# One feed-forward stage of an eight-stage kernel: the activation clip moved from VectorE to ScalarE, the 8-bit rounding read from PSUM, and a quarter of the last butterfly level moved into TensorE's Hadamard product

## The reference

```
def act_quant(x):                      # per token, 8 bits
    scale = 128 / clip(max|x|, 1e-5)
    return clip(round(x * scale), -128, 127) / scale
def weight_quant(w):                   # ternary, one scale
def fwht(x):                           # Walsh-Hadamard over the last axis, h = 1, 2, 4 ... n/2
    a, b = pairs at distance h;  x = [a + b, a - b];  ...;  x / sqrt(n)

gate = act_quant(x) @ weight_quant(w_gate).T          # 256 -> 1024
up   = act_quant(x) @ weight_quant(w_up).T
mid  = silu(gate) * up
out  = act_quant(fwht(mid)) @ weight_quant(w_down).T  # 1024 -> 256
```

## Time and profile before

| | us |
|---|---|
| three runs | 1581.56, 1587.24, 3211.22 |
| their median | 1587.24 |
| span of the profiled execution | 1593.2 |
| the stage in it, from the first `rstd` to the next stage's first | 263.5 to 420.2 |
| POOL busy in 291 to 404 | 109.0 of 113 |

### The profile page before, as it was taken

The page is one execution under the profiler, slowest core; times in us unless marked ns, Lnnn a source line. Parts: engine busy times, 40 slices in busy tenths (PEclk is TensorE's granted clock), DMA queues, the critical chain, the costliest instruction groups (busy, mean ns, idle before and its releaser), DMA issues. The chain is left out here.

```text
span 1593.2 us, 29325 instructions
## 1 busy us (share of the span) xinstructions
PE 1359.9 (85%) x7991; PEld 850.6 (53%) x7992; DVE 1047.0 (66%) x2409; ACT 795.0 (50%) x2354; POOL 633.9 (40%) x658
## 2 busy tenths in 40 slices
PE   5889995778689697999979999888995999968993
PEld 3555552555444253675545666564663666654661
DVE  5898886787568746224648888844334888864224
ACT  4676763666500045331028888723442888833330
POOL 3113411999477313760021111114435664214661
PEclk9999997999899689999979999958997999998997
DMA  5130002300100230985100000421442111412224
GB/s 188 49 107 23 22 9 94 122 0 0 53 0 0 60 115 14 287 283 173 52 28 23 23 26 22 163 64 47 130 121 80 48 53 33 172 54 63 83 82 165
DMA packets 96447, 124.80 MB, mean 78 GB/s; under 512 B 11117, under 2 KB 76464, under 8 KB 96112
## 3 DMA queue, kind: packets, MB, share of 16 engines
q1 hardware_dynamic: 85760, 95.80, 18.9%
q0 software_dynamic: 10608, 28.07, 6.1%
HBM read 91.31 MB, written 33.43 MB: 78 GB/s over the span
## 5 line engine op out<-in xcount | busy, mean ns | idle before, releaser
L717 ACT ACTIVATE l0a_prob<-l0a_ps_s,l0a_neg_max 128x128 f32<-128x128 f32 x512 | 137.9, 398 | 70.8 <-DVE l0a_neg_max L559 63.2
L717 ACT ACTIVATE l2a_prob<-l2a_ps_s,l2a_neg_max 128x128 f32<-128x128 f32 x512 | 138.7, 402 | 26.7 <-DVE l2a_neg_max L559 22.0
L1160 ACT ACTIVATE l3a_prob<-l3a_ps_s,l3a_neg_max 128x256 f32<-128x256 f32 x256 | 104.5, 483 | 33.0 <-DVE l3a_neg_max L1074 31.5
L219 POOL TENSOR_TENSOR ln_rstd<-ln_var_eps,minus_half 128x4 f32<-128x4 f32 (+1 forms) x14 | 23.1, 1656 | 238.9 <-POOLq L183 208.7
L559 DVE TENSOR_REDUCE l2a_neg_max<-l2a_ps_s 128x4 f32<-128x512 f32 x128 | 85.7, 684 | 20.5 <-PE l2a_ps_s L815 19.6
L502 POOL TENSOR_TENSOR l2a_k_head<-l2a_kT,head_of_row 128x512 f32<-128x512 f32 x32 | 33.1, 1054 | 158.0 <-DMA l2a_kT<-k_rows 158.0
L568 DVE COPY l0a_probT<-l0a_ps_t 128x512 f32<-128x512 f32 x128 | 84.7, 683 | 14.5 <-PE l0a_ps_t L827 14.4
L1074 DVE TENSOR_REDUCE l3a_neg_max<-l3a_ps_s 128x2 f32<-128x512 f32 x128 | 84.0, 680 | 13.4 <-PE l3a_ps_s L1211 12.4
L559 DVE TENSOR_REDUCE l0a_neg_max<-l0a_ps_s 128x4 f32<-128x512 f32 x128 | 85.5, 683 | 8.2 <-PE l0a_ps_s L815 7.5
L502 POOL TENSOR_TENSOR l0a_k_head<-l0a_kT,head_of_row 128x512 f32<-128x512 f32 x32 | 32.6, 1040 | 137.9 <-DMA l0a_kT<-k_rows 137.9
L1819 PE MATMUL l1a_ps_y<-l1a_kv,l1a_tap 128*128 128x512 f32 x192 | 84.1, 601 | 3.7 <-POOL l1a_kv L1791 3.7
(11 more groups left out here) (475 smaller groups left out, 3543.1 us busy)
## 6 DMA issues: line engine op xcount, KB each, us to landing
l1f_w_gu<-in_l1f_w_gu SPq DMA_DIRECT2D x32, 352.0 KB, 6.5
expert_results<-zeros SPq DMA_DIRECT2D x1, 8320.0 KB, 26.3
l1f_got<-expert_results SPq DMA_DIRECT2D x16, 512.0 KB, 4.4
expert_results<-l2f_y_sb SPq DMA_DIRECT2D x47, 128.0 KB, 1.7
l1f_w_d<-in_l1f_w_d SPq DMA_DIRECT2D x32, 176.0 KB
l2f_w_gu_all<-in_l2f_w_gu SPq DMA_DIRECT2D x1, 4096.0 KB, 14.1
l3f_w_gu_all<-in_l3f_w_gu SPq DMA_DIRECT2D x1, 4096.0 KB, 14.0
l3f_got<-expert_results SPq DMA_DIRECT2D x16, 256.0 KB, 5.5
```

The source lines that it names most:

```text
L717: last = act.activation(prob[4 * c + j][:, r * P:r * P + P], ps_s[j][:, r * P:r * P + P], ACT.Exp, bias=neg_max[:, j, r:r + 1])
L1160: last = act.activation(prob[4 * c + j][:, m * D:m * D + D], ps_s[j][:, m * D:m * D + D], ACT.Exp, bias=neg_max[:, j, m:m + 1])
```

## The change

- `clip_x` goes from DVE to ACT. DVE did `min(xr - MAGIC, 127)`; ACT now does `relu(MAGIC + 127 - xr)`, which is 127 minus that value, and the copy of `xqT` out of PSUM (before a plain copy) now does `127 - value`. In ACT's tile it stands last, after `norm`, for tile `t+4`; DVE had it first in its tile, for `t+3`.
- `round_h` writes back into `ps_f` (PSUM) instead of an SBUF buffer, and `quantise_h` on DVE reads `ps_f`. PE may refill `ps_f` only when `hq` is done, where before it was when the rounding was done.
- The two factors `deq` are written by two 128x1 instructions instead of one 128x2. There are two `a_rec` buffers, with a wait of DVE on the rounding two tiles back.
- POOL's levels come in the order 512, 256, 128 columns apart. The last level is done for blocks 0 to 5 only (two instructions of 128x384 instead of 128x512); the difference that becomes blocks 6 and 7 is written straight into `mixed` by the level before. PE does the missing pair: for block 6 it multiplies by `[H H]`, for block 7 by `[H -H]`, each 256 columns wide, summed in PSUM.
- The Hadamard matrix is loaded twice side by side, and ACT makes the negative once, before the stage's first work. Two more constants are set on POOL.

```diff
@@ load_ahead
-        sp.dma_start(core.had[:, :], core.dram["had"]).then_inc(core.had_in, 16)
+        sp.dma_start(core.had[:, 0:2, :], core.dram["had"].unsqueeze(1).broadcast_to([P, 2, P])).then_inc(core.had_in, 16)
@@ POOL
-            pool.memset(magic[:, :], MAGIC).then_inc(const_done, 1)
+            for n, value in ((magic, MAGIC), (clip_at, MAGIC + 127.0), (top_level, 127.0)):
+                pool.memset(n[:, :], value).then_inc(const_done, 1)
...
-                for n, (src, dst) in enumerate(((prod[u], fly), (fly, prod[u]), (prod[u], mixed[u]))):
-                    v, o = (m[:, :].rearrange("p (a two c) -> p a two c", two=2, c=P << n) for m in (src, dst))
-                    if n:
-                        pool.drain()
-                    pool.tensor_tensor(o[:, :, 0, :], v[:, :, 0, :], v[:, :, 1, :], ALU.add)
-                    last = pool.tensor_tensor(o[:, :, 1, :], v[:, :, 0, :], v[:, :, 1, :], ALU.subtract)
-                last.then_inc(mixed_done, 1)
+                even, odd = pairs(prod[u], W4)
+                high, low = pairs(fly[:, :], W4)
+                pool.tensor_tensor(high, even, odd, ALU.add)
+                pool.tensor_tensor(low, even, odd, ALU.subtract)
+                pool.drain()
+                even, odd = pairs(fly[:, :], 2 * P)
+                pool.tensor_tensor(pairs(prod[u], 2 * P)[0], even, odd, ALU.add)
+                pool.tensor_tensor(levels[u][:, :].rearrange("p (n c) -> p n c", c=2 * P)[:, 1:8:6, :], even, odd, ALU.subtract)
+                pool.drain()
+                even, odd = pairs(prod[u][:, 0:6 * P], P)
+                high, low = pairs(mixed[u][:, 0:6 * P], P)
+                pool.tensor_tensor(high, even, odd, ALU.add)
+                pool.tensor_tensor(low, even, odd, ALU.subtract).then_inc(mixed_done, 1)
@@ DVE
-                dve.reciprocal(a_rec[:, :], a_max[u][:, :]).then_inc(x_scaled, 1)
-                dve.tensor_scalar(deq[u][:, :], w_mean[:, 0:2], a_max[u][:, :], None, ALU.mult)\
-                   .then_inc(deq_done, 1)
-
-            def clip_x(t):
-                dve.wait_ge(x_rounded, t + 1)
-                if after(t, 1):
-                    dve.wait_ge(xqT_put, t)
-                dve.tensor_scalar(xq[:, :], xr[:, :], MAGIC, 127.0, ALU.subtract, ALU.min).then_inc(xq_done, 1)
+                if after(t, 2):
+                    dve.wait_ge(x_rounded, t - 1)
+                dve.reciprocal(a_rec[u][:, :], a_max[u][:, :]).then_inc(x_scaled, 1)
+                for n in range(2):
+                    dve.tensor_scalar(deq[u][:, n:n + 1], w_mean[:, n:n + 1], a_max[u][:, :], None, ALU.mult)\
+                       .then_inc(deq_done, 1)
...
-                dve.tensor_scalar(hq[:, :], rounded[:, :], MAGIC, 127.0, ALU.subtract, ALU.min).then_inc(hq_done, 1)
+                dve.tensor_scalar(hq[:, :], ps_f[:, :], MAGIC, 127.0, ALU.subtract, ALU.min).then_inc(hq_done, 1)
@@ ACT
+            def clip_x(t):
+                act.wait_ge(x_rounded, t + 1)
+                if after(t, 1):
+                    act.wait_ge(xqT_put, t)
+                act.activation(xq[:, :], xr[:, :], ACT.Relu, bias=clip_at[:, :], scale=-1.0).then_inc(xq_done, 1)
...
-                act.activation(xqT[u][:, :, :].rearrange("p c t -> p (c t)"), ps_xqT, ACT.Copy).then_inc(xqT_done, 1)
+                act.activation(xqT[u][:, :, :].rearrange("p c t -> p (c t)"), ps_xqT, ACT.Identity, bias=top_level[:, :],
+                               scale=-1.0).then_inc(xqT_done, 1)
...
-                if after(t, 1):
-                    act.wait_ge(hq_done, t)
-                act.activation(rounded[:, :], ps_f[:, :], ACT.Identity, bias=magic[:, :], scale=b_rec[:, :])\
+                act.activation(ps_f[:, :], ps_f[:, :], ACT.Identity, bias=magic[:, :], scale=b_rec[:, :])\
                     .then_inc(round_done, 1)
...
                 if ahead(t, 5):
                     norm(t + 5, 1 - u)
+                if ahead(t, 4):
+                    clip_x(t + 4)
@@ PE
-                        pe.wait_ge(round_done, t)
-                for c in range(half * NF // 2, (half + 1) * NF // 2):
-                    last = pe.matmul(ps_f[:, c * P:c * P + P], mixedT[:, c * P:c * P + P], had[:, :], start=True, stop=True)
+                        pe.wait_ge(hq_done, t)
+                for c in range(half * NF // 2, (half + 1) * NF // 2 - 2 * half):
+                    pe.matmul(ps_f[:, c * P:c * P + P], mixedT[:, c * P:c * P + P], had[:, 0, :], start=True, stop=True)
                 if half:
+                    for n in range(2):
+                        last = pe.matmul(ps_f[:, 6 * P:8 * P], mixedT[:, (6 + n) * P:(7 + n) * P],
+                                         had[:, n:n + 2, :].rearrange("p n c -> p (n c)"), start=(n == 0), stop=(n == 1))
                     last.then_inc(had_put, 1)
```

More of the change, by code:

```diff
@@ L143, in __init__ @@
         self.ffn_raw = [self.sb(f"ffn_raw{n}", [P, KC * FF], F32, self.early) for n in range(3)]
-        self.had = self.sb("had_matrix", [P, P], F32, self.early)
+        self.had = self.sb("had_matrix", [P, 3, P], F32, self.early)
         self.w_int = [self.sb(f"w_int{n}", [P, KC * FF], BF16, self.early) for n in range(3)]
@@ L1305, in hadamard_ffn @@
         had = core.had
-        magic = sb("magic", [P, 1])
+        magic, clip_at, top_level = (sb(n, [P, 1]) for n in ("magic", "clip_at", "top_level"))
         xn = [sb(f"xn{u}", [P, D]) for u in range(2)]
@@ L1311, in hadamard_ffn @@
         xqT = [sb(f"xqT{u}", [P, KC, P], BF16) for u in range(2)]
-        a_max, a_rec = [sb(f"a_max{u}", [P, 1]) for u in range(2)], sb("a_rec", [P, 1])
+        a_max, a_rec = ([sb(f"{n}{u}", [P, 1]) for u in range(2)] for n in ("a_max", "a_rec"))
         deq = [sb(f"deq{u}", [P, 2]) for u in range(2)]
@@ L1316, in hadamard_ffn @@
         gate = sb("gate", [P, FF])
-        prod = [sb(f"prod{u}", [P, FF]) for u in range(2)]
+        levels = [sb(f"levels{u}", [P, 2 * FF]) for u in range(2)]
+        prod, mixed = ([b[:, n * FF:n * FF + FF] for b in levels] for n in range(2))
         fly = sb("fly", [P, FF])
-        mixed = [sb(f"mixed{u}", [P, FF]) for u in range(2)]
         mixedT = sb("mixedT", [P, FF])
-        rounded = sb("rounded", [P, FF])
         hq = sb("hq", [P, FF], BF16)
@@ L1339, in hadamard_ffn @@
             "rstd_done", "shift_done", "normed", "x_scaled", "x_rounded"))
-        zeroed = sem("zeroed")
+        zeroed, had_ready = sem("zeroed"), sem("had_ready")
         block = st.enter_context(nc.Block())
@@ L1359, in butterflies, with pairs @@
                     pool.wait_ge(mixT_put, t - 1)
-                for n, (src, dst) in enumerate(((prod[u], fly), (fly, prod[u]), (prod[u], mixed[u]))):
-                    v, o = (m[:, :].rearrange("p (a two c) -> p a two c", two=2, c=P << n) for m in (src, dst))
-                    if n:
-                        pool.drain()
-                    pool.tensor_tensor(o[:, :, 0, :], v[:, :, 0, :], v[:, :, 1, :], ALU.add)
-                    last = pool.tensor_tensor(o[:, :, 1, :], v[:, :, 0, :], v[:, :, 1, :], ALU.subtract)
-                last.then_inc(mixed_done, 1)
+                def pairs(m, width):
+                    v = m.rearrange("p (a two c) -> p a two c", two=2, c=width)
+                    return v[:, :, 0, :], v[:, :, 1, :]
+                even, odd = pairs(prod[u], W4)
[11 more added lines that the diff above has]
+                pool.tensor_tensor(low, even, odd, ALU.subtract).then_inc(mixed_done, 1)
             over_tiles(pool, butterflies)
@@ L1423, in tile @@
             def tile(t, u):
-                if ahead(t, 3):
-                    clip_x(t + 3)
                 if ahead(t, 2):
@@ L1462, in round_x @@
                     act.wait_ge(xq_done, t)
-                act.activation(xr[:, :], xn[u][:, :], ACT.Identity, bias=magic[:, :], scale=a_rec[:, :])\
+                act.activation(xr[:, :], xn[u][:, :], ACT.Identity, bias=magic[:, :], scale=a_rec[u][:, :])\
                     .then_inc(x_rounded, 1)
+            def clip_x(t):
[3 more added lines that the diff above has]
+                act.activation(xq[:, :], xr[:, :], ACT.Relu, bias=clip_at[:, :], scale=-1.0).then_inc(xq_done, 1)
             def copy_xqT(t, u):
@@ L1469, in copy_xqT @@
                     act.wait_ge(up_put, t - 1)
-                act.activation(xqT[u][:, :, :].rearrange("p c t -> p (c t)"), ps_xqT, ACT.Copy).then_inc(xqT_done, 1)
+                act.activation(xqT[u][:, :, :].rearrange("p c t -> p (c t)"), ps_xqT, ACT.Identity, bias=top_level[:, :],
+                               scale=-1.0).then_inc(xqT_done, 1)
             def silu(t, u):
                 act.wait_ge(gate_put, t + 1)
-                act.wait_ge(deq_done, t + 1)
+                act.wait_ge(deq_done, 2 * t + 2)
                 if after(t, 1):
@@ L1512, in tile @@
                     norm(t + 5, 1 - u)
+                if ahead(t, 4):
+                    clip_x(t + 4)
+            act.wait_ge(core.had_in, 16)
```

(9 more changed lines are left out.)

3 lines of the change are left out of this document (removed).

## The result

| | before | with the change |
|---|---|---|
| median of 19 runs each | 1584.56 us | 1600.82 us |
| ratio | | 1.0093, 95% interval 1.0072 to 1.0114 |
| span of the profiled execution | 1593.2 | 1599.1 |
| the stage in it, first `rstd` to the next stage's first | 156.63 | 170.29 |

One run on each side was far slower (3211.22 and 2270.51 us), and the ratio leaves these two out. It makes 14.7 us, with its interval 11.4 to 18.1, on 1584.56; the two medians are 16.3 apart; the forecast was +13.9. The stage in the profile is 13.66 longer.

What follows compares the result with a forecast made beforehand. It took a circle of hand-offs of 8.28 us per tile through ACT, DVE and PE, without POOL, as the bound. 6.4 (clip) + 7.2 - 0.2 (PE) + 0.5 (end) = +13.9 on 1587.2 gave 1601 us, range 1589 to 1612.

Steps and rivals of the forecast that it cites:

- The bound: A circle of hand-offs among ACT, DVE and PE sets the stage's period of 8.28 us; POOL is not in it.
- POOL as the bound: Rival, 10%: the stage follows POOL's 7.12 us per tile, 15 periods x 1.0 = -15 us, total 1572.
- The circle: From second copy of mixedT through silu, product, maximum, reciprocal, rounding, round_x, norm and first copy to the next: 8.28 us.
- POOL and the port costed at nothing: POOL's 8.12 to 7.12 us per tile and DVE's vanished port waits gain nothing, being off the circle.
- Clip on ACT: One more ACT instruction between norm and the first copy: 13 x 0.49 = 6.4 us, bounds 3.6 to 7.8.
- PE: Transform's second half with 256-column products: 0.45 us per tile, 16 x 0.45 = 7.2, less 0.2 in the first tile.
- Rounding in PSUM: round_h on ACT writing PSUM: taken as 0, with bounds of +-3.3 us in all.
- The end: At the stage's end nothing covers the slower quantise_h from PSUM: +0.5 us.
- The third rival: The clock falls, 4%: longer waits keep PE at 1.2 GHz, 15 x 2.5 = 37 us more, total 1638.
- Additions hidden: Rival, 10%: clip and wider PE columns fall in gaps, only the 0.5 us at the end is paid, total 1588.
- A table load per relu: Rival: ACT reloads its table for relu in every tile; excluded by the order, with the unforeseen 2%.

Runs made afterwards that it cites:

- the relief of POOL alone: Kernel before, with POOL's last butterfly level left out on blocks 6 and 7 and nothing put on PE; stage 156.8 us, period 8.28, run ratio 1.0011.
- the clip in a gap: Changed kernel with ACT's clip of tile t+3 put between the two copies of hqT; stage 164.3 us, period 8.70, ratio 1.0028 to the kernel before.
- the butterfly part alone: Kernel before with only POOL's last level on 6 of 8 blocks and PE's two products of 256 columns; stage 163.4 us, period 8.70, ratio 1.0043.
- the three instructions in gaps: Changed kernel with round_x, clip_x and norm moved into ACT's gaps; stage 160.1 us, period 8.09, ratio 1.0024 to the kernel before.
- the first with the early turn: Changed kernel with round_x, clip_x, norm in ACT's gaps, and mixedT's next first half turned and copied early; stage 156.4 us, period 8.04.
- The first with the early turn and the old butterflies: The early-turn kernel with POOL doing the whole last level again and PE's products at 128 columns; stage 152.2 us, period 7.81.
- the two with the cut first: Early-turn kernels with DVE's cut of h ahead of the sum into x: stage 150.0 us with 256-column products, 152.4 with the old butterflies.

## Why the prediction was right

*The bound.* Right, and shown by the relief of POOL alone (+0.2) against the -9 to -10 that POOL as the bound would have given. The circle's length, 8.28, came back in the kernel that left its members alone (8.28) and in the one that, of its members, changed only where the rounding is written (8.27). POOL's row before was less unbroken than it looked: it paused 0.24 before its second tile, and in twelve tiles one of its instructions took 0.45 longer than the others, which in a timeline shows as work and not as a gap:

```profile
343.25 1.72 POOL L1365 TENSOR_TENSOR l0f_prod<-l0f_fly 128x512 f32<-128x512 f32 x1
```

With the cut of `h` from PSUM and the narrow factors alone, the same instruction took 1.27 throughout the steady part, and so it did with the change. So a busy share of 97% held some waiting too; POOL's own work before was about 7.7 us per tile.

*POOL and the port costed at nothing.* Right. The idle time of POOL is 1.78 to 2.05 per steady period, forecast about 2; `deq` is 0.32 for the pair, 194 to 206 ns each in all 32, so it waits nowhere; the cut from PSUM is 1.21 (forecast 1.22). The Trainium skill, SBUF — State Buffer (Who interferes with whom), describes such waits as an exclusive lock on ports that VectorE shares with GpSimd, and leaves out of it a VectorE instruction with at most one SBUF input outside its two-port modes; that the cut of `h` from PSUM is free of them beside a busy POOL agrees (`hq` 1.21 in every period, where the old form took 0.69 alone and 1.02 beside it). Here the waits did not matter.

*Clip on ACT.* The mechanism right, the size too high: 0.39 in the circle, where 0.49 had been taken. The instruction is 0.50 long, not 0.59 as its neighbours, and gives way 0.10 before its end as they do. 12 x 0.39 = 4.7 instead of 6.4. The thirteenth, before the first tile, is there too, 0.40 between clip and copy, but it is not paid: with DVE rid of its own cuts the last rounding in the start came 0.36 earlier, 19.60 us after the stage's start instead of 19.96, and the copy at 21.00 instead of 20.96. The clip alone shows the same (19.58 and 20.98). The prediction had left DVE's relief in the start out. Before, and with the change:

```profile
283.50 0.60 ACT L1463 ACTIVATE l0f_xr<-l0f_xn,l0f_magic,l0f_a_rec 128x256 f32<-128x256 f32 x1 [2.79 <-DVE l0f_a_rec L1382]
```

```profile
286.58 0.60 ACT L1465 ACTIVATE l0f_xr<-l0f_xn,l0f_magic,l0f_a_rec 128x256 f32<-128x256 f32 x1 [2.79 <-DVE l0f_a_rec L1394]
287.58 0.49 ACT L1472 ACTIVATE l0f_xq<-l0f_xr,l0f_clip_at 128x256 bf16<-128x256 f32 x1
287.98 0.57 ACT L1492 ACTIVATE l0f_mixedT<-l0f_ps_t 128x512 f32<-128x512 f32 x1
```

*PE.* 0.43 against 0.45: from the start of the second half to the maximum 1.57 instead of 1.14. 15 x 0.43 = 6.5, where 7.2 less 0.2 was forecast; what the first tile paid is in the 0.18 by which the start grew.

*Rounding in PSUM.* 1.18 against 1.20, and the next instruction on ACT starts 1.10 after it in both: the unknown of +-3.3 was worth nothing. Its bounds came from 0.59 against 0.38 for 256 columns, read as SBUF against PSUM. At least part of that is another thing: the copy of `xqT` went from 0.38 to 0.47 when it was given a bias, still from PSUM.

*The end.* +0.5, as forecast.

*What wasn't in the sum.* The clock fell once more, near the end of the stage. After a stretch of 2 us in which PE was busy for 0.75, the granted clock fell to 0.50, the lower level of 1.2 GHz, at 416 to 418:

```profile
412.00:414.00 2.00, 0.75 (x5) 0.42 (x4) 1.81 (x3) 1.27 (x2) 2.00 (x2) 1.00 0.00 0
414.00:416.00 2.00, 1.33 (x10) 1.27 (x11) 0.02 (x1) 0.60 (x1) 1.86 (x3) 0.88 0.00 0
416.00:418.00 2.00, 2.00 (x10) 1.85 (x9) 0.00 (x0) 0.60 (x1) 0.51 (x1) 0.50 0.00 0
```

The two products of 256 columns took 1.90 there instead of 1.03, and that period is 9.39 long beside 7.72 for the next: +1.6. The kernel before had the upper level at that point of its tail. PE's busy time just before doesn't settle the cause: with the clip in a gap it was busy for 0.76 at 402 to 404, with the clock at 1.00 there and in the next 6 us, and for 0.76 again at 410 to 412, with a fall behind it. The third rival was this, kept to one period instead of the whole stage.

The sum as measured: 4.7 + 6.5 + 0.2 + 0.5 + 1.6 = 13.5 of 13.66. Two errors of about 1.6 us, the clip too dear and the clock not seen, cancel in the 13.9; the forecast is nearer than it had a right to be. That the time itself came within 0.2 of the 1601 is luck on top of it: the forecast stood on 1587.2 for the kernel before, whose median is now 1584.56. The three parts alone make the same sum, 6.1 + 6.8 + 0.7 = 13.6, but not from the same terms: none of the three has the late period, while the clip alone paid 0.8 at its end and the butterfly part alone 0.65 in its start, where the change paid 0.5 and 0.2. In the steady periods, all at the upper clock, the parts do add up: 8.67 and 8.70 less 8.28 are 0.39 and 0.42, together 0.81 of the 0.82.

*The rivals.* POOL as the bound: refuted. Additions hidden: refuted, both are in the period to the hundredth. A table load per relu: the profile has one load in the stage, as before.

## What to carry to other kernels

An engine that is busy 97% of a stage need not be its bound: before relieving it, add up the hand-offs from one instruction to the same instruction of the next tile, through all engines, and see whether the circle is as long as the period. If it is, only what stands in the circle counts, in both directions: the same 0.5 us instruction cost 0.39 per tile at one place of ACT's order and nothing at another, and the relief of POOL was worth nothing until the circle had been shortened from 8.28 to 7.6, and then 0.11 per tile. A buffer that is now held longer (PSUM read by the cut) is a wait in store: it cost nothing at 9.10, with 1.1 us to spare, and set the period at 8.13.

## What the runs showed of the hardware

- A ScalarE instruction with an f32 source in SBUF, a bias and a constant scale, writing bf16 took 0.50 us for 256 columns, beside 0.59 for two that take scale and bias from SBUF and write f32. Part of it is likely the second operand read from SBUF: the copy of `xqT`, 256 columns from PSUM, took 0.38 without a bias and 0.47 with a bias from SBUF and a constant scale, and of the rest only the function changed, from Copy to Identity. What the types and the function add was not tested.
- ScalarE writing 1024 columns back into the PSUM tile that it reads took 1.18 us, against 1.20 to an SBUF tile.
- One or two late periods of 8.8 to 9.4 stand in the profiles of the change, of its kernels with the clip or the three instructions in gaps, and of the first with the early turn, each with a mean PE clock of 0.57 to 0.62 over 4 us from the start of the transform there. The first with the early turn and the old butterflies has a smaller one, 7.86 before 6.88, at 0.62. The kernel before, the four with one part alone and the two with the cut first show none. What brings the clock down at that place was not tested; where the period behind it is at the upper level again (9.39 before 7.72, 8.84 before 7.18), it costs 1.7 us.
